# Reordering the attention head of a fused layer-and-adapters kernel: turns of one half between another half's turns and products

## The reference

```python
attn = softmax((x@Wq) @ (x@Wk).T * V**-0.5)
attn_out = (attn @ (x@Wv)) @ Wp + bp
cms = gelu(attn_out @ cW1 + cb1) @ cW2 + cb2 + one_hot(codes)
mod = gelu(concat(attn_out, cms) @ mW1 + mb1) @ mW2 + mb2
x = clip(x + cms + mod, 0, 1)
for layer in range(3):        # r = role of the batch, one of 3
    h = gelu(x @ W_down[layer][r] + b_down[layer][r])
    x = layernorm(x + h @ W_up[layer][r] + b_up[layer][r]) * gamma[r] + beta[r]
```

## Time and profile before

| | us |
|---|---|
| median of 3 runs | 358.4 |
| lowest and highest of them | 358.2, 358.91 |
| the profiled execution | 357.08 |
| its span, on which all rows count | 355.2 |
| PE busy in the span | 344.4 |
| DVE, ACT, POOL busy | 202.6, 169.2, 62.0 |

### The profile page before, as it was taken

One profiled execution on the slowest core, in us unless ns is written; L12 is line 12 of the kernel. 1 busy time (PEld: TensorE's weight loads), 2 busy tenths in 40 slices (PEclk: granted clock), 3 DMA queues, 4 the chain that ended last, 5 costly groups with the idle time before them and its releaser, 6 DMA issues.

```text
span 355.2 us, 6665 instructions
## 1 busy us (share of the span) xinstructions
PE 344.4 (97%) x2252; PEld 287.1 (81%) x2252; DVE 202.6 (57%) x488; ACT 169.2 (48%) x338; POOL 62.0 (17%) x94
## 2 busy tenths in 40 slices
PE   7799999999999999999999999999999999999994
PEld 6587678787878888888886777877899999999962
DVE  5066375433353875466545666554589777554584
ACT  3555685453642563463336454443455544543421
POOL 2700230000040110012311111003322024100231
PEclk9999998999999999999999999999999999999998
DMA  6674899284020141310075898412856533188001
GB/s 211 199 221 146 206 126 144 57 192 109 2 54 6 60 119 62 101 49 6 25 253 163 226 257 306 104 31 74 227 145 188 168 104 108 59 273 345 23 2 45
DMA packets 30646, 46.14 MB, mean 130 GB/s; under 512 B 4779, under 2 KB 15348, under 8 KB 30612
## 3 DMA queue, kind: packets, MB, share of 16 engines
q1 hardware_dynamic: 28852, 41.72, 43.0%
q0 software_dynamic: 1392, 3.80, 3.9%
q10 hardware_dynamic: 368, 0.20, 0.2%
HBM read 43.60 MB, written 4.48 MB: 135 GB/s over the span
## 4 chain that ended last, share of the span: by engine, by line
PE 91%; ACT 3%; DVE 2%; issue 2%; POOL 1%; POOLq 0%; DVEq 0%
PE bank L332 12%; PE bank L334 12%; PE bank L333 12%; PE bank L1437 9%; PE bank L1442 8%; PE bank L1438 8%; PE bank L1481 4%; PE bank L1460 4%; PE bank L1343 2%; PE bank L1361 2%; PE bank L1512 2%; PE bank L1301 2%; PE bank L1242 1%; PE bank L1560 1%; PE bank L1457 1%
## 5 line engine op out<-in xcount | busy, mean ns | idle before, releaser
L798 ACT ACTIVATE h_full<-bank,bias 128x512 f32<-128x512 f32 (+1 forms) x80 | 48.2, 603 | 108.3 <-PE bank L334 98.0
L1035 DVE TENSOR_TENSOR h_lo<-h_full,h_hi 128x512 fp32r<-128x512 f32 (+1 forms) x80 | 46.8, 585 | 63.2 <-ACT h_hi L802 60.8
L718 POOL TENSOR_TENSOR rstd<-moments,minus_half 128x1 f32<-128x1 f32 x39 | 24.3, 623 | 168.1 <-DVE moments L1101 167.9
L802 ACT ACTIVATE h_hi<-h_full 128x512 fp32r<-128x512 f32 (+1 forms) x80 | 43.7, 547 | 2.5
L1093 DVE TENSOR_TENSOR window_y<-bank,window_x 128x256 f32<-128x256 f32 x39 | 16.5, 423 | 38.3 <-PE bank L1460 28.9
L1437 PE MATMUL bank<-h_hi,c_hi 128*128 128x512 f32 (+1 forms) x80 | 30.8, 393 | 0.2
L1437 PE MATMUL bank<-h_hi,m_hi 128*128 128x512 f32 (+1 forms) x80 | 30.2, 387 | 0.2
L332 PE MATMUL bank<-at_hi,c_hi 128*128 128x512 f32 (+1 forms) x80 | 29.3, 366 | 0.0
L332 PE MATMUL bank<-at_hi,m_hi 128*128 128x512 f32 (+1 forms) x80 | 29.2, 364 | 0.0
L334 PE MATMUL bank<-at_lo,c_hi 128*128 128x512 f32 (+1 forms) x80 | 27.9, 348 | 0.0
L334 PE MATMUL bank<-at_lo,m_hi 128*128 128x512 f32 (+1 forms) x80 | 27.8, 348 | 0.0
(11 more groups left out here) (239 smaller groups left out, 733.9 us busy)
## 6 DMA issues: line engine op xcount, KB each, us to landing
adapter_w<-packed_w SPq DMA_DIRECT2D x44, 256.5 KB, 3.5
adapter_rows<-packed_rows SPq DMA_DIRECT2D x36, 256.0 KB, 5.2
stage<-in_L_cond_mW SPq DMA_DIRECT2D x6, 512.0 KB, 6.3
mixed_w<-packed_w SPq DMA_DIRECT2D x8, 256.5 KB, 5.0
stage<-in_L_cond_cW SPq DMA_DIRECT2D x4, 512.0 KB, 4.7
last_w<-packed_w SPq DMA_DIRECT2D x2, 769.5 KB, 6.4
up_bias<-in_L_cond_b_up SPq DMA_DIRECT2D x12, 128.0 KB, 6.1
adapter_rows<-packed_rows SPq DMA_DIRECT2D x24, 64.0 KB
```

Of the source, the lines that this page charges most:

```text
L718: pool.tensor_tensor(slot.rstd[:, :], slot.moments[:, 1:2], minus_half[:, :], ALU.pow)\
L798: act.activation(h_full[:, n % 2, rows], bank[n % 2][:, rows], ACT.Gelu, bias=bias[:, b:b + 1])\
L802: act.activation(h_hi[:, n % 2, rows], h_full[:, n % 2, rows], ACT.Copy).then_inc(h_hi_ready, 1)
L1035: dve.tensor_tensor(h_lo[:, n % 2, rows], h_full[:, n % 2, rows], h_hi[:, n % 2, rows].bitcast(F32), ALU.subtract).then_inc(h_lo_ready, 1)
```

## The change

Five edits, all in the head:

1. On PE, X of half 2 stands ahead of Y of half 1, and Y of half 2 ahead of S of group 0. On ACT the copies follow: X of half 2 ahead of Y of half 1, and each chunk's copy one place later than before (chunk 1 behind Y of half 1, chunk 2 behind Y of half 3, chunk 3 behind the exponential of group 1).
2. EARLY goes from 3 to 1: one chunk is asked for at once, the second waits for halves 0 and 1, the third for halves 2 and 3.
3. DVE's wait ahead of the first chunk's low part goes.
4. A new tile `filler`, set to 1.0 by DVE as its first instruction, takes the place of `ident` in the unused products. PE waits for it, and for `ident` only ahead of the weights' turns.
5. Four unused products stand at the opening instead of two, and a narrow one (32 columns) behind the role product.

```diff
-EARLY = 3
+EARLY = 1
...
+        filler = sb("filler", [P, P])
...
# ACT
             half_part("X", 0)
-            chunks(1, 2)
             half_part("Y", 0)
             half_part("X", 1)
+            half_part("X", 2)
             half_part("Y", 1)
-            half_part("X", 2)
+            chunks(1, 2)
+            half_part("Y", 2)
             half_part("X", 3)
             attention_part("S", 0)
-            chunks(2, 4)
-            half_part("Y", 2)
             half_part("Y", 3)
+            chunks(2, 3)
             attention_part("Z", 0)
             attention_part("S", 1)
+            chunks(3, 4)
             attention_part("B", 0)
...
# DVE
+            dve.memset(filler[:, :], 1.0).then_inc(pd_clear, 1)
...
-                    dve.wait_ge(pd_clear, 2)
+                    dve.wait_ge(pd_clear, 3)
...
-            dve.wait_ge(half_turned, 3)
             chunks(0, 1)
...
# PE
-            pe.wait_ge(ident_ready, 1)
+            pe.wait_ge(pd_clear, 1)
...
-                    pe.matmul(bank[6][:, 0:columns], ident[:, :], ident[:, 0:columns], start=True, stop=True)
-
-            keep_busy(2)
+                    pe.matmul(bank[6][:, 0:columns], filler[:, :], filler[:, 0:columns], start=True, stop=True)
+
+            keep_busy(4)
...
             pe.matmul(bank[4][0:B, 0:1], role_row[:, 1, :], ones[0:1, 0:1], start=True, stop=True).then_inc(roles_turned, 1)
+            keep_busy(1, P // 4)
...
+            pe.wait_ge(ident_ready, 1)
             turn_weights(0)
...
             half_part("X", 1)
+            half_part("X", 2)
             half_part("Y", 1)
-            half_part("X", 2)
+            half_part("Y", 2)
             attention_part("S", 0)
             half_part("X", 3)
-            half_part("Y", 2)
             half_part("Y", 3)
```

## The result

The changed kernel takes 361.83 us (median of 6 executions, 358.35 to 362.71), the kernel before, on the same chips, 358.25 us (6 executions, 357.08 to 358.91). The ratio is 1.0091, 95% interval 1.0053 to 1.013: slower, as forecast, but by some 3.6 us instead of 1.6, and 0.6 us past the end of the range. Of the later runs, one execution of e18 and three of the kernel before ran over 1.5% above the fastest of their kernel and are left out of every comparison.

The account below looks back on a forecast made before the run. PE was taken to bound the kernel, passing the head's loss to the end: −1.63 + 1.73 − 0.36 + 0.85 + 1.01 = +1.60 us, so 360.0 us against the 358.4 median. The range was 358.1 to 361.2 us.

Parts of the forecast that it names:

- What bounds, and the order's cost: PE holds 91% of the chain; the head's loss passes to the end; first hidden product comes 1.60 us later.
- The wait at Z0: Group 0's context on PE waits for the softmax probabilities' transposes, 1.0 us after PE was ready.
- The landing of half 2: Half 2's rows usable 2.15 us after the sixth transfer's end on GpSimd; its turns start at 18.0 against 19.63.
- The upper bound for X2: Latest start of half 2's turns on PE, 18.3 us, giving +1.9 us.
- The opening: Longer unused work on PE at the start may lift the clock sooner: 0.1 us gained, bounds −0.1 to +0.25.
- VectorE's wait removed: First chunk's subtraction overlaps a gather's start by 0.36 us, costing 0.2 by the trace's measure; taken 0.1.
- stretched in full: Rival: subtraction just under way as transfer 4 or 5 starts; halves 2 and 3 come 1.0 us later, 361.0; chance 0.12.
- The clock, on the other side: Rival: PE's clock falls in the wait before half 2's turns, another 1.7 us, 361.7; chance 0.04.
- The clock, on the faster side: Rival: clock fall near 60 us absent, 1.7 us saved: 358.4, chance 0.12; with an opening gain 357.6, chance 0.11.
- signs of being wrong: Half 2's turns before 17.3, context straight behind half 3's products, clock 1.00 at 60 to 64, first hidden product by 33.2.
- The sum: Whole kernel: 357.08 us profiled plus 1.6 makes 358.7; against the median of 358.4, 360.0 us.

Follow-up runs that it names:

- e18: Changed kernel with the second chunk's load behind all four halves, VectorE's wait restored, and 8 unused products between half 1's and half 2's turns: 360.28 us, ratio 1.0049.
- e10: Kernel before with the new order of halves alone (EARLY 3, VectorE's wait and old opening kept): 360.22 us, ratio 1.0094.
- e5: Changed kernel with the old order of halves on PE and ACT, all else as changed: 357.91 us, ratio 1.0017.
- e2: Changed kernel with 8 unused 128-column products between half 1's and half 2's turns: 360.08 us, ratio 1.0079.
- e8: Changed kernel with the second chunk's load behind all four halves and VectorE's wait restored: 358.84 us, ratio 1.0037.
- e11: Kernel before with the new opening alone (four unused products, a narrow one behind the role product): 358.34 us, ratio 1.0035.
- e14: Changed kernel run again unaltered, to examine its head: 360.87 us, ratio 1.0105.
- e4: Changed kernel with the second chunk's load waiting for all four halves instead of two, its copy moved behind the first exponential: 359.49 us, ratio 1.0077.
- e7: Changed kernel with VectorE's wait ahead of the first chunk's low part put back: 360.69 us, ratio 1.0095.
- e6: Changed kernel with half 2's products put back behind group 0's scores and half 3's turns: 359.59 us, ratio 1.0055.
- e1: Changed kernel run again unaltered, to see what its times are made of: 360.31 us, ratio 1.0106.
- e15: Changed kernel with VectorE's wait restored and the second chunk's load cut into four pieces: 357.14 us in a single execution, no ratio.
- e17: Changed kernel with 14 unused 128-column products between half 1's and half 2's turns: 362.57 us, ratio 1.0118.
- e12: Kernel before's order and VectorE's wait, EARLY 2, next chunk's load behind all four halves, four unused opening products without the narrow one: 357.07 us, ratio 0.9982.
- e13: Kernel before, unaltered, run and profiled again: 357.12 us, ratio 1.0002.

## Why the prediction was right and where it fell short

**What bounds, and the order's cost: right.** PE led the chain, the head's loss was passed on, and the loss is the order's (e10 1.0094, e5 1.0017). The passing on can be read in all 20 profiles: from H0 to the end of the span it is 320.2 to 322.2 us in the six without a fall of the clock around 60 us, 322.0 to 323.9 in the twelve with one, and 324.0 and 324.1 in e2 and e18, whatever H0 is (32.6 to 37.6). Every start from X2 to H0 came in the order and with the waits that were written down: Y3 0.69 us idle behind ScalarE's copy, Z0 held by the transposes. X2 to H0 took 16.57 us, forecast 16.76.

**The wait at Z0: somewhat too long.** Forecast 1.0 us. PE could have started Z0 at 25.18 + 1.73 = 26.91 and did at 27.52: 0.6. The exponential came 1.19 us behind X3 instead of 1.31, and Z0 followed the transposes (26.21 + 1.25 = 27.46) by 0.06 instead of 0.32.

**The landing of half 2: the term that was mis-sized.** The step took 2.15 us, the middle between 1.9 and 2.4, with the remark that the load issued at 15.26 "is still there in both kernels". There lay the error: in the kernel before, X2 stood at 19.63 whatever half 2 did, so no row could show what that load does to rows landing at the same time. The 1.9 and 2.0 us of the earlier trace rows belong to transfers 3 and 7; transfer 3 lands before that load is issued. The one landing in the earlier trace rows with loads in flight, half 0's 2.4 us, served only for the upper bound. Measured: 3.0 with the load, 1.8 without (e8). That makes X2 19.09 instead of 18.0 (0.9 us by the landing, 0.2 by a later sixth transfer) and the head's cost 2.5 instead of 1.6. With the load out of the way, e8 gives H0 34.68 against the forecast 34.76, by the luck named above. The upper bound for X2, 18.3, should have been open to a landing just before 19.63, the last moment that the trace of before allows.

**The opening: no gain.** Taken as 0.1 gained, with −0.1 as the bound; in the profile the first transfer starts 0.2 later, and e11 is at 1.0035 (1.0 to 1.0069). The narrow product, which puts the counting 0.17 us back, was left out of the sum; how much of the 0.2 is its doing is open, as that start varies by 0.46 us with the old opening.

**VectorE's wait removed: the measure was right, the place is not fixed.** A transfer that starts while the subtraction is under way grows by nearly what of it is left: 0.05 us left, nothing (after); 0.65 left, 0.5 (e14, 1.47 instead of 0.95); 0.88 left, 0.7 (e2, 1.69); 1.14 left, 1.0 (e4, 1.97). The forecast's 0.2 for 0.36 lies on that line, but the subtraction started between 13.72 and 14.78 in these profiles, so that it met the transfers elsewhere each time. e7 shows that keeping the wait doesn't pay either while the load is in flight (1.0095). The rival "stretched in full" was thus what happened in the profiles of e4 and e6, half of it in e14, and none of it in the first profile.

**The clock: the rival with the smallest chance is part of the miss.** "The clock, on the other side", 0.04, priced at +1.7, is what e1 and e14 show, two of the three profiles of the changed kernel, and the price was about right: from X2 to H0 e14 takes 18.25 us and e1 17.95, against 16.57 at full clock, so 1.7 and 1.4 more. The argument against it was that PE was idle for 1.8 us from 12 to 18 us in before at a granted clock of 1.00. That was one execution, with idle times of at most 0.74 us each; the changed kernel waits 2.5 us at a stretch. The Trainium skill (TensorE: Matmul & The Clock Gate, section HAM oscillation — how this bites in real kernels) describes a case of this kind, a wait for a DMA, longer than the products ahead of it, after which the next products start at the lower clock. The traces of e1 and e14 show such a fall, at 0.72 from 18 to 24 us; that of the first profile, which waited 0.3 us longer than e14's, does not, nor does that of e6, which waited longest of all (2.99 us).

**The clock, on the faster side**, was true of the profiled execution (1.00 from 59 to 64 us, one of the signs of being wrong that the prediction named), but it does not go with the change: from 60 to 66 us e14 has 0.85 and e1 0.75. It helps explain why the profile's time, 358.35, is at the low end.

**The sum.** At like clock about +2 us where +1.6 was forecast, and some +1.7 us by a clock that stands low more often, a term that the forecast put at nothing. The range ended at 361.2 because a later landing and a fall in the wait were treated as rivals, one or the other; in e1 and e14 both came together, and 361.83 is past the price of each alone. Why the clock stands low more often stays open.

## What to carry to other kernels

Before a consumer of gathered rows is moved forward, look at what else is in flight when they land: a landing that the trace shows only as "no later than its use" has no upper bound but that use. A reorder that puts a new wait on TensorE may cost its clock too (here in two of eight profiles with waits of 1.2 to 3.0 us), so price the wait and the fall together, not only as rivals. Where single executions differ by 2 us, read the granted clock of each before reading the profile of one, and profile the kernel before more than once: its two heads differ by 1.5 us.

## What the runs showed of the hardware that I had not expected

- An indirect transfer's rows were usable 1.8 to 1.9 us after the instruction's end on GpSimd without a chunk load beside them (e4, e8; half 0 in e6 and e15), 2.4 to 3.4 us with one or more loads of 512 KB, and once 4.7 (e17).
- The time at which PE begins to work at full pace varies from execution to execution. The first eight products with the weights, begun at 7.8 to 8.3 us, took 2.0 to 3.1 us in 18 profiles and 3.78 in e12 and e13. In e12 the second set of weight products still ran at half pace, though the granted clock of the stretch reads 1.00. Its row on PE, to set beside 1.99 us for the same eight at 10.70 in the kernel after:

```profile
12.80 3.78 PE L1242 MATMUL bank<-raw,wT 128*128 128x256 f32 x8
```

  and the stretch around them:

```profile
12.00:18.00 6.00, 5.34 (x23) 3.72 (x23) 0.78 (x3) 2.84 (x6) 4.48 (x6) 1.00 0.35 107
```

  So a granted clock of 1.00 in the first microseconds of these profiles doesn't say that PE runs at full pace; the duration of a known form does. X0 stood at 16.69 there, against 12.7 to 14.8 in the other profiles.
- The subtraction with two inputs in SBUF stretches a transfer that starts during it by nearly its remaining time, up to 1.0 us, and doesn't stretch one that started 0.08 us ahead of it.
- Filling PE's wait with 14 unused products went with a mean clock of 0.9952, against 0.9906 without and 0.9954 in the kernel before, and gained no time (1.0118).
